# Expert gate weights spread to 64 partitions by transfers from DRAM rows instead of by a selector product

## What is computed

```
x = whiten(x) * g0 + b0                # statistics over all tokens, groups of 16 channels
t = tokens of x
t = t + layernorm(window_attention(layernorm(t))) * g1 + b1v     # 33 neighbours
u = layernorm(t)
logits = u @ router_w.T                # 8 experts
combine[n, e] = weight of expert e for token n, zero but for the top 2
out = t + u + sum over e of combine[:, e] * (gelu(u @ w1[e] + b1[e]) @ w2[e] + b2[e])
```

## Time and profile before

| | |
|---|---|
| median of 3 runs | 1266.45 us (1265.63 to 1267.43) |
| profiled execution, its own time | 1265.46 us |
| span of the profiled execution, first to last instruction | 1263.6 us |
| mean granted TensorE clock | 0.916 of 2.4 GHz |
| TensorE busy | 1141.2 us, 90% |
| VectorE busy | 1018.8 us, 81% |
| ScalarE busy | 672.6 us, 53% |
| GpSimd busy | 211.2 us, 17% |
| HBM read, written | 39.81 MB, 25.69 MB |

### The profile page before, as it was taken

The page is one execution under the profiler, slowest core; times in us unless marked ns, Lnnn a source line. Parts: engine busy times, 40 slices in busy tenths (PEclk is TensorE's granted clock), DMA queues, the critical chain, the costliest instruction groups (busy, mean ns, idle before and its releaser), DMA issues.

```text
span 1263.6 us, 27959 instructions
## 1 busy us (share of the span) xinstructions
PE 1141.2 (90%) x8762; PEld 795.0 (63%) x8762; DVE 1018.8 (81%) x3482; ACT 672.6 (53%) x1183; POOL 211.2 (17%) x217
## 2 busy tenths in 40 slices
PE   7867888898888887898975999999999999999998
PEld 7846777787767776777864555555555555555554
DVE  6848889899898999989887887777777777777775
ACT  0025655565655655565643556555555655555663
POOL 5012333333333333333332000000000000000000
PEclk9959987887988989888885999999999999999999
DMA  9401111111111111111011111112111111212111
GB/s 332 146 15 38 46 45 44 44 47 42 44 44 44 44 44 44 44 44 44 30 37 37 30 44 44 44 44 47 47 46 48 44 44 44 49 45 51 44 44 37
DMA packets 127771, 66.15 MB, mean 52 GB/s; under 512 B 111104, under 2 KB 125696, under 8 KB 126944
## 3 DMA queue, kind: packets, MB, share of 16 engines
q1 hardware_dynamic: 119024, 52.26, 15.9%
q10 hardware_dynamic: 8064, 12.85, 2.7%
q0 software_dynamic: 624, 0.43, 0.1%
HBM read 39.81 MB, written 25.69 MB: 52 GB/s over the span
## 4 chain that ended last, share of the span: by engine, by line
PE 52%; DVE 37%; issue 4%; POOL 3%; ACT 3%; DMA 1%; ACTq 0%; POOLq 0%; DVEq 0%; SPq 0%
PE p L1074 15%; PE p L1049 14%; PE p L1059 9%; DVE xn_s L766 7%; DVE t_s L760 6%; DVE tn_s L775 5%; POOL t_s L406 3%; PE p L901 3%; DVE arena L614 3%; DVE st L720 3%; PE p L894 2%; PE p L997 2%; DVE sm L734 2%; PE p L1070 2%; PE p L988 2%
## 5 line engine op out<-in xcount | busy, mean ns | idle before, releaser
L822 DVE TENSOR_TENSOR arena<-arena,p 128x896 f32<-128x896 f32 x224 | 243.5, 1087 | 129.2 <-PE p L1059 124.0
L539 ACT ACTIVATE arena<-p,b_s 128x896 f32<-128x896 f32 x224 | 224.8, 1005 | 228.5 <-PE p L1049 228.5
L1074 PE MATMUL p<-arena,w_s 128*64 128x448 f32 x896 | 215.3, 559 | 0.3 <-DVE arena L822 0.3
L1049 PE MATMUL p<-thl,w_hi 128*128 128x448 f32 x448 | 165.0, 449 | 0.4 <-DVE thl L796 0.4
L1059 PE MATMUL p<-arena,selector 128*128 128x448 bf16 x448 | 124.4, 360 | 3.4 <-DVE arena L822 2.9
L1049 PE MATMUL p<-thl,w_lo 128*128 128x448 f32 x448 | 127.5, 365 | 0.0
L1059 PEld LDWEIGHTS p<-arena,selector 128*128 128x128 bf16 x448 | 25.5, 97 | 161.1 <-issue 115.8
L1017 PE MATMUL p<-arena 128*96 128x128 f32 x784 | 107.0, 277 | 0.0
L1017 PEld LDWEIGHTS p<-arena 128*96 128x96 f32 x784 | 102.1, 169 | 4.0
L406 POOL TENSOR_TENSOR t_s<-t_s,yb 128x448 f32<-128x448 f32 x56 | 63.5, 1134 | 213.8 <-DVE tn_s L775 213.4
L1049 PEld LDWEIGHTS p<-thl,w_hi 128*128 128x128 f32 x448 | 85.6, 192 | 21.2 <-issue 0.8
(11 more groups left out here) (164 smaller groups left out, 2033.3 us busy)
## 6 DMA issues: line engine op xcount, KB each, us to landing
tn_spill<-tnt_s ACTq DMA_DIRECT2D x56, 224.0 KB, 1.9
arena<-tn_spill SPq DMA_DIRECT2D x56, 224.0 KB, 3.4
arena<-in_x_dram SPq DMA_DIRECT2D x112, 96.0 KB, 2.1
out_dram<-arena SPq DMA_DIRECT2D x112, 96.0 KB, 1.8
resid<-in_x_dram SPq DMA_DIRECT2D x6, 1568.0 KB, 12.2
resid<-in_x_dram SPq DMA_DIRECT2D x6, 384.0 KB, 6.3
arena<-in_x_dram SPq DMA_DIRECT2D x112, 16.0 KB, 2.1
out_dram<-arena SPq DMA_DIRECT2D x112, 16.0 KB, 1.7
```

Source lines behind the costliest of these rows:

```text
L539: a.activation(hid[:, j % 2, :].rearrange("p (h n) -> p h n", h=H), (p34 if j % 2 == 0 else p56)[:, :, 0:CH], ACT.Gelu, bias=b1_s[:, j:j + ...
L822: v.tensor_tensor(gated[:, j % 2, :].rearrange("p (h n) -> p h n", h=H), hid[:, j % 2, :].rearrange("p (h n) -> p h n", h=H), p01[:, :, 0: ...
L1049: last = t.matmul(bank[:, h, 0:CH], w[:, 128 * j:128 * (j + 1)], thl[:, c, h, :], start=(k == 0), stop=(k == 1))
L1074: last = t.matmul(p2[64 * h:64 * h + 64, 0:CH], w2_s[:, j, :], gated[:, j % 2, h * CH:(h + 1) * CH], start=False, stop=(j == 3))
```

## The change

The selector product is dropped, and with it `comb_t`, the bf16 split, `ct_copy` and `double`. The gate weights go through DRAM:

- `route` writes an image's weights in an order that puts the seven chunks of an image beside each other. During the seven drain steps of stage 2, and once after chunk 4 of stage 3 for the last image, `turn_gates` on TensorE turns one whole image's weights (eight fp32 matmuls into `p01`), and `spill_gates` on ScalarE copies them to SBUF and stores them to a DRAM tensor with one row of 896 tokens for each chunk and expert.
- SP loads for every chunk and quarter two such rows, each repeated over 64 partitions, into one of four buffers (`gates`). The buffer is free when `gate` of the same quarter of the chunk before is done. It also loads the chunk's eight rows once more into partitions 64 to 71 of `tn_in`, where they serve as the operand of the bias product.
- `gate` multiplies in place in `hid`, which now has four buffers; both inputs are in SBUF. The four-deep `hid` replaces `hid` and `gated` with two each.
- The bias product is two fp32 matmuls with `b2_w` instead of four bf16 ones.
- The order of SP's issues changes, as shown.

The diff, cut to its core:

```diff
@@ sync: stage 3
-            def step3(g, c, has):
-                if has(0):
-                    wait(sp, s_hi, g - 1)
-                    wait(sp, s_lo, g - 1)
-                    sp.dma_start(tn_in[:, c, :].rearrange("p (h n) -> p h n", h=H),
-                                 spill[g].rearrange("(h p) n -> p h n", h=H)).then_inc(s_ti[c], 16)
-                if has(2):
-                    wait(sp, s_fin, g - 1)
-                    for tile, tokens in pieces(out_tokens, g - 2, fin[:, c, :]):
-                        sp.dma_start(tokens, tile).then_inc(s_out[c], 16)
+            def tokens_in(g, c):
+                wait(sp, s_hi, g - 1)
+                wait(sp, s_lo, g - 1)
+                wait(sp, s_l2, 4 * (g - 2) + 1)
+                sp.dma_start(tn_in[0:64, c, :].rearrange("p (h n) -> p h n", h=H),
+                             spill[g].rearrange("(h p) n -> p h n", h=H)).then_inc(s_ti[c], 16)
+            def rows_in(g, c):
+                wait(sp, s_l2, 4 * (g - 2) + 1)
+                sp.dma_start(tn_in[64:64 + E, c, :], shares[g]).then_inc(s_ci[c], 16)
+            def gates_in(g, j):
+                wait(sp, s_gm, 4 * (g - 1) + j + 1)
+                for e in range(2):
+                    sp.dma_start(gates[j][64 * e:64 * e + 64],
+                                 shares[g, 2 * j + e].partition_broadcast(64)).then_inc(s_gi[j], 16)
+            def store(g, c):
+                wait(sp, s_fin, g + 1)
+                for tile, tokens in pieces(out_tokens, g, fin[:, c, :]):
+                    sp.dma_start(tokens, tile).then_inc(s_out[c], 16)
+            def step3(g, c, ahead=True):
+                gates_in(g, 0)
+                gates_in(g, 1)
+                if not isinstance(g, int) or g >= 2:
+                    store(g - 2, c)
+                gates_in(g, 2)
+                if ahead:
+                    tokens_in(g + 1, 1 - c)
+                    rows_in(g + 1, 1 - c)
+                gates_in(g, 3)
@@ sync: constants, start and end of stage 3
-                             (rank[:, :], k_rank.partition_broadcast(128)), (sel_f[:, :], k_sel),
+                             (rank[:, :], k_rank.partition_broadcast(128)),
+            for im in range(1, NP - 1):
+                sp.wait_ge(s_cd2[im % 2], 32 * (im // 2 + 1))
@@ gpsimd, in the drain
-                if c == 2:
+                if c == 3:
                     pool.wait_ge(s_s, G)
-                    v.memset(ct_s, 0.0)
-                    v.memset(cparts, 0.0).then_inc(s_zero, 1)
+                    pool.wait_ge(s_res, G)
+                    v.memset(tn_in[64:128], 0.0).then_inc(s_zero, 1)
@@ scalar
-                wait(act, s_gm, u - 1)
-                a.activation(hid[:, j % 2, :].rearrange("p (h n) -> p h n", h=H),
+                wait(act, s_l2, u - 3)
+                a.activation(hid[:, j, :].rearrange("p (h n) -> p h n", h=H),
-            def double(g, c):
...
+            def spill_gates(im):
+                k = im % 2
+                act.wait_ge(s_ct, im + 1)
+                wait(act, s_cd2[k], 32 * (im // 2))
+                a.activation(turned[k], p01[:, 1, 0:CH], ACT.Copy).then_inc(s_cts, 1)
+                act.wait_ge(s_cts, im + 1)
+                for h in range(H):
+                    act.dma_start(shares[im * CPI:(im + 1) * CPI, :, h * CH:(h + 1) * CH].rearrange("k e n -> (k e) n"),
+                                  turned[k][64 * h:64 * h + CPI * E]).then_inc(s_cd2[k], 16)
@@ vector: comb in another order; ct_copy and parts_step are gone
-                    v.tensor_tensor(comb[:, bass.ds(im * (T * E), T * E)].rearrange("p (t e) -> p t e", e=E),
-                                    pick[:, 0], pick[:, 1], ALU.add).then_inc(s_comb, 1)
+                    v.tensor_tensor(comb[:, bass.ds(im * (T * E), T * E)].rearrange("p (t k e) -> p k t e", t=NB, k=CPI),
+                                    pick[:, 0].rearrange("p (k t) e -> p k t e", k=CPI),
+                                    pick[:, 1].rearrange("p (k t) e -> p k t e", k=CPI), ALU.add).then_inc(s_comb, 1)
             def gate(g, c, j):
-                wait(dve, s_g, u + 1)
-                wait(dve, s_c, u + 1)
-                wait(dve, s_l2, u - 1)
-                v.tensor_tensor(gated[:, j % 2, :].rearrange("p (h n) -> p h n", h=H),
-                                hid[:, j % 2, :].rearrange("p (h n) -> p h n", h=H),
-                                p01[:, :, 0:CH], ALU.mult).then_inc(s_gm, 1)
+                wait(dve, s_g, g * 4 + j + 1)
+                wait(dve, s_gi[j], 32 * (g + 1))
+                v.tensor_tensor(hid[:, j, :], hid[:, j, :], gates[j], ALU.mult).then_inc(s_gm, 1)
@@ tensor: comb_t and spread are gone
+            def turn_gates(im):
+                pe.wait_ge(s_comb, im + 1)
+                wait(pe, s_cts, im)
+                of = comb[:, im * NB * CPI * E:(im + 1) * NB * CPI * E].rearrange("p (t n) -> p t n", t=NB)
+                for b in range(NB // 2):
+                    for h in range(H):
+                        t.matmul(p01[64 * h:64 * h + CPI * E, 1, b * 128:(b + 1) * 128], of[:, 2 * b + h, :], eye[:, :],
+                                 start=True, stop=True)
...
             def second_layer(g, c, j):
                 if j == 0:
                     wait(pe, s_y3s, g)
-                    for p in range(2):
-                        for h in range(H):
-                            t.matmul(p2[64 * h:64 * h + 64, 0:CH], b2_p[:, p, C * h:C * h + C], ct_s[:, c, :],
-                                     start=(p == 0), stop=False)
+                    wait(pe, s_ci[c], 16 * ((g // 2 if isinstance(g, int) else cur["pair"]) + 1))
+                    for h in range(H):
+                        t.matmul(p2[64 * h:64 * h + 64, 0:CH], b2_w[:, :], tn_in[:, c, h * CH:(h + 1) * CH],
+                                 start=True, stop=False)
@@ drain steps, tensor and scalar
             for c in range(7):
                 step(G + c, c, lambda d, c=c: d > c)
+                pe.wait_ge(s_ys, G)
+                turn_gates(c)
...
                 step(G + c, c, lambda d, c=c: d > c)
+                spill_gates(c)
```

More of the change, by code:

```diff
@@ L164, in hybrid_kernel @@
         at3 = [0]
-        tn_in = carve(at3, [2, H * CH], rows=64)
-        hid = carve(at3, [2, H * CH])
-        gated = carve(at3, [2, H * CH])
+        tn_in = carve(at3, [2, H * CH])
+        hid = carve(at3, [4, H * CH])
         y3 = carve(at3, [CH])
         fin = carve(at3, [2, CH])
[L170 to L173, removed]
+        gates = [carve(at3, [H * CH])]
+        assert at3[0] <= ARENA - 3 * NB * CPI * E
         with nc.sbuf_tensor("yb", [128, CPI, CH], f32) as yb:
@@ L194, in hybrid_kernel @@
         top = sb("top", [128, 5, NB * CPI])
+        gates.append(yb_tail[:, 0:H * CH])
+        gates.extend(tile[:, 0:H, :, :].rearrange("p s b c -> p (s b c)") for tile in (t_s, tn_s))
+        turned = [xt_s[:, :], xn_s[:, :, :].rearrange("p b c -> p (b c)")]
         p01 = pb("p01", [128, 2, 512])
@@ L322, in _ @@
+            sp.wait_ge(s_zero, 3)
+            sp.wait_ge(s_cd2[0], 32)
+            for c in range(2):
+                rows_in(c, c)
+            sp.wait_ge(s_s, G)
+            gates_in(0, 0)
+            sp.wait_ge(s_t2, G)
+            gates_in(0, 1)
+            sp.wait_ge(s_res, G)
+            gates_in(0, 2)
+            sp.wait_ge(s_tnt, G)
+            gates_in(0, 3)
             for k in range(3):
@@ L324, in _ @@
                 sp.wait_ge(s_sp[k], 16 * spilled)
-            sp.wait_ge(s_s, G)
-            with sp.Fori(1, G // 2) as i:
-                for c in range(2):
-                    step3(i * 2 + c, c, lambda d: True)
-            for c in range(2):
-                step3(G + c, c, lambda d: d > 0)
+            for im in range(1, NP - 1):
+                sp.wait_ge(s_cd2[im % 2], 32 * (im // 2 + 1))
+            gates_in(1, 0)
+            gates_in(1, 1)
+            gates_in(1, 2)
+            tokens_in(2, 0)
+            rows_in(2, 0)
+            gates_in(1, 3)
+            for g in range(2, 8):
+                step3(g, g % 2)
+            sp.wait_ge(s_cd2[(NP - 1) % 2], 32 * ((NP - 1) // 2 + 1))
+            with sp.Fori(4, G // 2 - 1) as i:
+                for c in range(2):
+                    step3(i * 2 + c, c)
+            step3(G - 2, 0)
+            step3(G - 1, 1, ahead=False)
+            store(G - 2, 0)
+            store(G - 1, 1)
             for c in range(2):
@@ L838, in step3 @@
                                 finish(g - 1, 1 - c)
-                        if j == 3 and more:
-                            ct_copy(g + 1, 1 - c)
                         gate(g, c, j)
@@ L1051, in first_layer @@
                 last.then_inc(s_h, 1)
-            def spread(g, c, j):
-                u = g * 4 + j
-                if j == 0:
-                    wait(pe, s_ctd, g + 1)
-                wait(pe, s_gm, u)
-                for h in range(H):
```

(12 more changed lines are left out.)

124 lines of the change are left out of this document (34 added, 90 removed).

## The result

The changed kernel takes 1317.71 us (median of 4 runs, 1316.8 to 1321.35) beside 1266.94 of the kernel before in the same comparison: the ratio is 1.0407, with an interval from 1.0385 to 1.0429. It is slower, by 51 us. The forecast was 1280: slower, by 14. The direction came, and so did the loop that was named as the cause; the size did not.

The account below looks back on a forecast made before the run. TensorE was taken to bound the old expert stage, SP's closed loop the new one: 1265.46 - 1.5 + 0.2 - 0.9 - 3.9 = 1259.4, plus 53 x 0.38 = 20.1, gives 1279.5, stated as 1280 us; range 1246 to 1325.

Parts of the forecast that it names:

- The closed loop: Expert stage: high, low, finish, stores, gate loads and tokens form one turn per chunk, 10.39 us against 10.01 before.
- tokens from issue to landing 3.4: Expert-stage loop: the 224 KB token load takes 3.4 us from SP's issue until it has landed.
- SP's own work: Expert stage: SP's issues and gaps take 10.1 us per chunk, with 0.50 per gate load.
- (a): Start of the kernel: the selector's 512 KB no longer load before the last part of x, -1.5 us.
- (b): Attention-stage drain: turning and spilling weights puts high(2) at 707.05 instead of 706.85, +0.2 us, bounds -4 and +4.
- (d): End after high(55): the chunk waits only for `low`, -3.0 us, and the last chunk has less work, -0.9.
- (c): Between high(2) and high(55): the last image's routing adds 2.0 us instead of 2.9, -0.9.
- (A): Rival: expert-stage loop shorter, SP issues near 0.35 to 0.42, 9.9 us per chunk, 1254 us; chance 0.17 of ending below 1263.
- (B): Rival: in the expert stage SP never lags and TensorE stays the bound, 8.7 us per chunk, 1193 us; chance 0.08.
- (C): Rival: expert-stage gate loads issue in 0.68, SP's own work of 11.5 us decides, 1339 or 1299 us; chance 0.17.
- (D): Rival: TensorE's clock falls to 0.87 in the expert stage, perhaps 0.3 us per chunk, 1297 us; chance 0.15.
- (E): Rival: repeated reads of one row run at half rate, DMA engines bound at some 12.5 us, 1390 us; chance 0.04.

Follow-up runs that it names:

- e2: Changed kernel plus one more 16 KB load on SP between the stores and the third pair of gate loads; 1354.63 us.
- e3: Changed kernel plus one more 16 KB load on SP between the second pair of gate loads and the wait for the stores; 1317.98 us.
- e10: Changed kernel with token and row loads ahead of the stores and of the third pair of gate loads, all on SP; 1254.92 us.
- e5: Changed kernel with each gate load bringing half the bytes from chunk 2 on, output not computed; 1290.36 us.
- e11: e7 with half the bytes per gate load from chunk 2 on, output not computed; 1208.49 us.
- e7: e6 with the token and row loads ahead of the third pair of gate loads; 1209.15 us.
- e4: Changed kernel with gate loads reading 64 different rows instead of one row 64 times, output not computed; 1312.26 us.
- e8: Changed kernel with one gate load to 128 partitions from different rows instead of two to 64, output not computed; 1306.89 us.
- e6: Changed kernel with the stores issued by ScalarE after gelu 3 instead of by SP; 1250.59 us.
- e1: Changed kernel with the four stores moved behind the chunk's last gate load on SP; 1283.48 us.

## Why the prediction was right and wrong

**The closed loop** was right in its place and in its members. e2 and e3 show that it is closed, e10 that it is what made the change slower: with the same issues in an order without it the changed kernel beats the one before.

**The step that failed is the token load's term of the loop, "tokens from issue to landing 3.4"**: too small, although the prediction named the load that would lengthen it. In the changed kernel it is 3.96 in the mean to `high`, 4.23 in the turn shown, where the sum has 3.45 with the hop. Against the turn at 899.06, part by part (forecast, measured): high to low 0.97, 0.98; low to finish 1.11, 1.12; finish to stores 0.79, 0.81; stores to gates 2 2.66, 2.81; gates 2 to tokens 1.41, 1.51; tokens to high 3.45, 4.23. Together 10.39 and 11.46, and of the 1.07 between them the tokens are 0.78. Over the whole stage the loop is 11.09 - 10.39 = 0.70 us longer than forecast, 37 us in 53 turns, and the tokens are 0.51 of it. The row was of a queue at a DMA share of 0.19. e5, with half the gate bytes, takes 0.55 us off, 29 of the 37 us, and has 3.43 to `high`. The prediction had the quantity as an end of the range ("tokens 1 us later, since they now share the engines with four times as many bytes") and took the unloaded value for its sum. The 11.09 measured lies within its bounds of 9.9 and 11.8 for the loop; what it got wrong is which value is the likely one. (The 9.9 is a slip: with issues of 0.34 and gaps of 0.12 throughout, the same sum gives about 9.8.) The Trainium skill's sentence on HBM access at high load (DMA: Bandwidth & Descriptors, Latency and other measured facts), which the prediction set aside for want of a row, pointed the right way: up to 1.8 us by it, 0.5 measured in the mean. No run separates slow memory from waiting in the queue.

**The stores and gaps** were 0.25 too short in the turn shown, all of it issue time. The changed kernel shows in itself what issuing costs in a loop: its chunks 2 to 7 are written out, with fixed addresses. The three issues of one such chunk, and below them the register work that SP does for line 325 (ns), which begins only at 774.4 us, where the loop over the other chunks does:

```profile
747.21 2.09 SPq L331 DMA_DIRECT2D out_dram<-arena  x4
749.34 1.24 SPq L325 DMA_DIRECT2D t_s<-gate_spill  x2
750.69 0.62 SPq L314 DMA_DIRECT2D arena<-tn_spill  x1
```

```profile
L325 SPq FUSED_REGOPS  x345: 37/37/48, 774.4 to 1286.4; - x173
```

From the stores' start to the gate loads' it is 2.13 there (2.1 to 2.4 in its neighbours) and 2.81 in the loop with register addresses, from the gate loads to the tokens 1.35 and 1.51. The turns from chunk 4 to chunk 8 take 10.4 to 10.6 us, those in the loop about 11.1. The prediction's rows came from a loop with register addresses too, so that this is no part of its miss beyond the 0.25; no run writes out more chunks to price it.

**SP's own work**, forecast 10.1, is 9.87 (e10). A gate load's issue, taken as 0.50 from the one broadcast row, is 0.47 to 0.54. The lines of L325 (ns, min/median/max), and its time from issue to landing:

```profile
L325 SPq DMA_DIRECT2D arena<-gate_spill x112: 466/473/611, 690.7 to 1297.4; - x112
...
L325 SPq DMA_DIRECT2D t_s<-gate_spill x112: 510/542/1455, 693.2 to 1305.7; - x112
...
DMA to landing us min/median/max: 3.2/4.1/7.1
```

**TensorE**, forecast 8.7 per chunk, is 8.9 to 9.0 (e11, e7). The bias product's two fp32 matmuls are as priced, four instructions. The removed work was real: in e7 it shows in the time. **The DMA engines** were priced at 7.2 us of engine time per chunk; the share of 0.82 says 0.82 x 11.4 = 9.3. They were no bound, as forecast, but what they had to move lengthened the landing.

**The ends.** (a) -1.5 for the selector's 512 KB did not come: the column sums end 0.7 us later instead of earlier, and the attention stage starts 0.2 us later. (b) 711.29 for high(2), where 707.05 was forecast: the token load of chunk 2 took 5.6 us, 2.2 more than 3.4, and the attention stage ran about 2.4 us later than before from its seventh chunk on. In e4 and e10, where that stage is the same code, its last store to `tn_spill` comes 1.7 and 1.5 us earlier than before; so the offset varies from execution to execution and need not come from the change. (d): after high(55) -2.9, forecast -3.9; (c) lies within the 53 turns. In the profiled execution, 1321.35 us against the forecast's 1279.5, the ends miss by 6.7 us ((a) included) and the turns by 35.1.

**Rivals.** (A) fell: the issues were not 0.35 to 0.42, but 0.47 to 0.54. (B) fell, since SP lags; its state, TensorE as the bound, is what e7 reaches with another order. (C) fell for the same 0.5. (D) fell as a price: the clock was 0.95, above the 0.87 that it took, and TensorE stands outside the loop. (E) fell by e4. Of the marks named for the trace, TensorE at 85%, `high` waiting for its tokens and 0.50 per gate load came; "SP issues nearly without a break" half, with 1.25 us idle per chunk; the DMA share was 0.82 instead of 0.7.

## What to carry to other kernels

Before work is moved from an engine to transfers, write down the issuing queue's order as a chain: whatever is issued behind a wait joins that wait's loop, and here the same 14 issues per chunk made 1318 or 1255 us by their order alone. Put loads that start the next round ahead of stores that end the last one, and give stores to a queue that has time (1209 us here). And take a transfer's landing time from a row at the load that the change will make, or, if there is none, put more on it than the unloaded row says. The DMA share alone does not give it: 224 KB took 3.4 us at a share of 0.19 and at 0.49, 4.0 at 0.82, 4.6 at 0.69 (e8), 4.4 at 0.98 (e6) and 5.6 at 0.99 (e10). In e10 and e7 (7.3 at 1.07) the load stood directly behind gate loads issued without a longer break, in e6 behind one pair after a wait. So look also at what stands ahead of it in its queue; that this is the reason was not tested by itself.

## What was not expected of the hardware

- A share of busy DMA engines near 1 is no ceiling. It was 0.94 in e1 at 225 GB/s and 1.07 in e7 at 259 GB/s; what grew was the time to landing.
- Register addresses lengthen SP's issuing, which has register work between the issues only there (37 ns each): stores followed by a pair of loads begin 2.13 us apart with fixed and 2.81 us apart with register addresses.
- Joining two loads of 64 partitions into one of 128 lowered the DMA share from 0.87 to 0.69 at equal GB/s, and the time by only 5 us, since the token load behind it landed 0.7 us later after asking.
- Reading one DRAM row 64 times is hardly slower than reading 64 rows: these were 5 us of 1318 faster.
